# Layer 0 of a two-layer transformer kernel: a new order of its pieces on five engines, with two pieces moved between engines

## What is computed

```python
x = x + tanh(g_xattn[0]) * L0_xattn(layernorm(x), ctx, masks, Wq, bq, Wk, bk, Wv, bv, Wo, bo)
x = x + tanh(g_ffn[0])   * L0_ffn(layernorm(x), w_up, w_down)
x = x + tanh(g_xattn[1]) * L1_xattn(layernorm(x), ctx, ...)
x = x + tanh(g_ffn[1])   * L1_ffn(layernorm(x), Wr, Win, Wout)

def L0_ffn(h, w_up, w_down):
    h = square(relu(hbitlinear(h, w_up)))
    return hbitlinear(h, w_down)
def hbitlinear(x, w):                       # fwht: a Hadamard transform
    return act_quant(fwht(x)) @ weight_quant(w).T
def act_quant(x):                           # per token, to 8 bits: "the grid"
    scale = 127 / max(abs(x)); return clip(round(x * scale), -127, 127) / scale
```

## Time and profile before

| | us |
|---|---|
| median of 3 executions (1254.0 to 1259.59) | 1256.76 |
| the profiled execution | 1250.93 |
| its span, first to last instruction | 1249.2 |
| PE / DVE / ACT / POOL busy in it | 1119.2 / 1024.9 / 944.2 / 748.0 |
| layer 0: start of F2 of the first and of the last row | 72.99 and 313.27 |

### The profile page before, as it was taken

One profiled execution on the slowest core, in us unless ns is written; L12 is line 12 of the kernel. 1 busy time (PEld: TensorE's weight loads), 2 busy tenths in 40 slices (PEclk: granted clock), 3 DMA queues, 4 the chain that ended last, 5 costly groups with the idle time before them and its releaser, 6 DMA issues. The chain is left out here.

```text
span 1249.2 us, 30643 instructions
## 1 busy us (share of the span) xinstructions
PE 1119.2 (90%) x8831; PEld 906.0 (73%) x8831; DVE 1024.9 (82%) x2453; ACT 944.2 (76%) x3793; POOL 748.0 (60%) x1142
## 2 busy tenths in 40 slices
PE   3589899978899999999999999998999999669992
PEld 2356566545788888888888888887887888559981
DVE  6678888887898898898889899888789887766664
ACT  4777788869999989989998998997888778223330
POOL 5378888867665665666566566665546787323331
PEclk8699999999999999999999999999999999879996
DMA  6655555531220230220221121122311010623326
GB/s 132 131 90 92 90 88 86 83 53 53 89 73 2 90 90 0 89 89 16 72 89 33 56 89 51 38 89 70 92 51 48 31 36 31 276 80 94 88 69 206
DMA packets 134168, 97.57 MB, mean 78 GB/s; under 512 B 54845, under 2 KB 127679, under 8 KB 134080
## 3 DMA queue, kind: packets, MB, share of 16 engines
q1 hardware_dynamic: 124528, 84.70, 27.0%
q0 software_dynamic: 3408, 8.45, 1.9%
q10 hardware_dynamic: 6144, 3.35, 0.9%
HBM read 55.02 MB, written 42.09 MB: 78 GB/s over the span
## 5 line engine op out<-in xcount | busy, mean ns | idle before, releaser
L1557 POOL TENSOR_TENSOR head_rstd<-head_rstd,minus_half 128x4 f32<-128x4 f32 x192 | 225.7, 1175 | 15.0
L1545 ACT ACTIVATE squares<-ps 128x128 bf16<-128x128 f32 x768 | 202.5, 285 | 42.3 <-PE ps L1508 35.1
L1508 PE MATMUL ps<-w_proj_in,xq 128*128 128x512 f16 (+1 forms) x1024 | 209.6, 327 | 6.0 <-ACT headsT L1581 5.4
L1637 POOL TENSOR_TENSOR prob<-prob,rinv 128x512 f32<-128x512 f32 x128 | 140.5, 1098 | 107.6 <-DVE rinv L1632 107.4
L1581 ACT ACTIVATE headsT<-ps,l_hln 128x256 f32<-128x256 f32 (+1 forms) x256 | 168.2, 691 | 29.3 <-PE ps L1572 29.2
L1624 ACT ACTIVATE prob<-ps,nmax 128x128 f32<-128x128 f32 x512 | 182.7, 392 | 9.2 <-DVE nmax L1615 7.8
L1545 ACT ACTIVATION_READ_ACCUMULATOR squares<-ps 128x1 f32 x768 | 165.4, 216 | 0.0
L1565 DVE TENSOR_TENSOR heads_n<-ps,head_rstd 128x512 f32<-128x512 f32 x192 | 131.1, 683 | 25.0 <-POOL head_rstd L1557 24.8
L1508 PEld LDWEIGHTS ps<-w_proj_in,xq 128*128 (+1 forms) x1024 | 99.9, 98 | 53.1 <-issue 8.8
L1608 PE MATMUL ps<-headsT 128*128 128x128 f32 x1024 | 136.2, 276 | 1.0 <-DVE probT L1653 0.4
L1555 POOL TENSOR_TENSOR head_rstd<-head_squares,l_head_eps 128x4 f32<-128x4 f32 x192 | 45.8, 238 | 151.9 <-ACT squares L1545 151.2
(11 more groups left out here) (321 smaller groups left out, 2611.3 us busy)
## 6 DMA issues: line engine op xcount, KB each, us to landing
slots<-blank_slot SPq DMA_DIRECT2D x12, 1554.0 KB, 8.0
halves<-half_made SPq DMA_DIRECT2D x32, 256.0 KB, 2.6
w_proj_in<-halves SPq DMA_DIRECT2D x16, 512.0 KB, 9.3
w_out_raw<-in_wprojT SPq DMA_DIRECT2D x8, 512.0 KB, 4.0
half_raw<-in_winT SPq DMA_DIRECT2D x16, 256.0 KB, 3.0
half_raw<-in_woutT SPq DMA_DIRECT2D x16, 256.0 KB, 3.1
taken<-slots SPq DMA_DIRECT2D x15, 259.0 KB, 3.5
q_rows<-q_parts SPq DMA_DIRECT2D x48, 64.0 KB
```

Source lines behind the costliest of these rows:

```text
L1508: last = e.matmul(out, xq[:, k, which, slot_at], weights(k, hl, c0, n), start=(k == 0 and hl == 0), stop=(k == KD - 1 and hl == 1))
L1545: last = e.activation(squares[:, 4 * n + h, :], A[n][:, h * HD1:(h + 1) * HD1], ACT.Square, scale=HD1**-0.5, accum_out=hss[:, 4 * n + h:4 ...
L1557: e.tensor_tensor(hr[:, four], hr[:, four], t["half"][:, four], ALU.pow).then_inc(g_r[n].sem, 1)
L1637: e.tensor_tensor(prob[:, kind, :, :], prob[:, kind, :, :], spread(rinv[:, kind, :], P), ALU.mult).then_inc(g_p[kind].sem, 1)
```

## The change

All orders in `ORDER0` are new. XB moves to a later place on GpSimd, F4v to a place behind F1g. F5v, WL and WC, which were one piece each, become two pieces each, with the same instructions. F6q keeps the four steps of the scale on VectorE; the two roundings become a new piece F6r on ScalarE, two activations with a wait between them. WM moves from ScalarE, where it was twelve instructions, to VectorE, where it is one reduction; it no longer writes to `w_proj_in` and no longer waits for WL. F7s waits for the scale instead of the rounded values. `starting` names other pieces for some of the first work, and the strings in `MIXED` are new.

```diff
 ORDER0 = {
     "tensor": (
-        "PV:2- PV:3- NT ST:5- P2t++ F6--- ST:6- OB:0- F2t-- ST:7- P3++ S:0+ F3-- PV:4- PV:5- PV:6- PV:7- ST:0 "
-        "S:1+ ST:1 S:2+ F4-- ST:2 OB:1- F4u-- S:3+ ST:3 S:4+ OT- ST:4 S:5+ F7--- W- S:6+ S:7+ F7d--- PV:0 "
-        "PV:1"
+        "P2t++ PV:2- S:7 PV:3- ST:5- F6--- ST:6- NT OB:0- P3++ ST:7- F2t-- S:0+ S:1+ PV:4- F3-- PV:5- PV:6- PV:7- "
+        "ST:0 ST:1 S:2+ OB:1- F4-- S:3+ F4u-- ST:2 S:4+ OT- ST:3 S:5+ F7--- W- PV:0 S:6+ ST:4 PV:1 F7d---"
+    ),
+    "vector": (
+        "MX:5+ Wv- MX:6+ F1- F7v--- MX:7+ WM++ F2- F6q-- NTl+ P1++++ NO:0 MX:0++ MX:1++ F3q- P3v+++ MX:2++ NO:1 "
+        "MX:3++ MX:4++ P2++++"
     ),
     "scalar": (
-        "EX:5 P2a+++ F2a- EX:6 EX:7 WM:0++ P3h+++ WM:1++ OC:1 EX:0+ EX:1+ F4a- EX:2+ F4s- OTa WH++ F7a-- EX:3+ NTh++ EX:4+ "
+        "P2a+++ EX:5 NTh+ EX:6 F2a- F6r-- EX:7 P3h+++ OC:1 EX:0+ F4a- EX:1+ F4s- OTa EX:2+ F7a-- EX:3+ EX:4+ WH++ "
         "OC:0+"
     ),
-    "vector": (
-        "MX:5+ Wv- MX:6+ MX:7+ F1- F7v--- NTl+ F2- F6q-- NO:0 P1++++ MX:0++ F3q- P3v+++ MX:1++ MX:2++ "
-        "NO:1 MX:3++ MX:4++ P2++++"
-    ),
-    "gpsimd": "XB+ F5v-- F1g- WL+ F3b- VC++ PD+ P1g++++ WC++ F7s-- F4v-",
+    "gpsimd": "F5v:0-- F5v:1-- F1g- F4v-- WL:0+ WL:1+ F3b- XB+ VC++ WC:0++ P1g++++ WC:1++ PD++ F7s--",
     "sync": "INS- ROW-- INT- LW OUT CT++",
 }
...
     @s.piece("F3", "tensor")
     def _(e, i, p):
         e.wait_ge(g_sum.sem, g_sum.at(i))
-        e.wait_ge(v_q2.sem, v_q2.at(i - 1))
+        e.wait_ge(a_g2.sem, a_g2.at(i - 1))
...
+    @s.piece("F6r", "scalar")
+    def _(e, i, p):
+        e.wait_ge(c_f6.sem, c_f6.at(i))
+        e.activation(rnd2[:, :], F1[:, :], ACT.Copy, bias=MAGIC, scale=quant[:, p, 6:7]).then_inc(a_g2.sem, 1)
+        e.wait_ge(a_g2.sem, a_g2.at(i, 1))
         e.wait_ge(pe_q2.sem, pe_q2.at(i - 1))
-        quantise(e, c_f6, quant[:, p, :], F1[:, :], quant[:, p, 7:8], 4, rnd2[:, :], q2[:, :], v_q2)
-        c_f6.end()
+        e.activation(q2[:, :], rnd2[:, :], ACT.Copy, bias=-MAGIC).then_inc(a_g2.sem, 1)
...
-    @s.piece("WM", "scalar")
+    @s.piece("WM", "vector")
+    def _(e, i, p):
+        e.wait_ge(d_unit.sem, d_unit.at(i))
+        e.tensor_reduce(wsum[:, p, :], unit[:, p, 0:CENTRED * HD1].rearrange("p (h d) -> p h d", h=CENTRED),
+                        AX, ALU.add).then_inc(v_usum.sem, 1)
...
-            ("gpsimd", "P1g", 1, 1): ("blocks",), ("gpsimd", "VC", 0, 0): ("more", "masks"), ("gpsimd", "WC", 0, 0): ("ready",),
-            ("gpsimd", "XB", 0, 0): ("gated",),
+            ("gpsimd", "P1g", 1, 1): ("blocks",), ("gpsimd", "VC", 0, 0): ("more", "masks"), ("gpsimd", "WC", 0, 0, 0): ("ready",),
+            ("gpsimd", "PD", 0, 0): ("gated",),
...
-            ("vector", "P1", 1, 1): ("ready", "unit0", "more"), ("vector", "P2", 1, 1): ("unit1",), ("vector", "P1", 2, 0): ("masks",),
-            ("vector", "NTl", 1, 1): ("late",), ("vector", "NO", 0, 0, 0): ("late2",),
+            ("vector", "P1", 1, 1): ("ready", "unit0", "more"), ("vector", "P2", 1, 1): ("unit1",), ("vector", "WM", 0, 0): ("masks",),
+            ("vector", "MX", 1, 1, 5): ("late",), ("vector", "NO", 0, 0, 0): ("late2",),
```

More of the change, by code:

```diff
@@ L65, in link, with last, at @@
         self.engine.wait_ge(self.sem, self.i * self.per + self.n)
+    def last(self, instruction):
+        instruction.then_inc(self.sem, 1)
+        self.n += 1
+    def at(self, i):
+        return i * self.per + self.per
     def end(self):
@@ L1024, in quantise @@
         chain.link(e.reciprocal(quant[:, c + 1:c + 2], quant[:, c:c + 1]))
-        chain.link(e.tensor_scalar(quant[:, c + 2:c + 3], quant[:, c + 1:c + 2], norm, 127.0, ALU.mult, ALU.mult))
+        step = e.tensor_scalar(quant[:, c + 2:c + 3], quant[:, c + 1:c + 2], norm, 127.0, ALU.mult, ALU.mult)
+        if done is None:
+            chain.last(step)
+            return
+        chain.link(step)
         chain.link(e.tensor_scalar(rnd, src, quant[:, c + 2:c + 3], MAGIC, ALU.mult, ALU.add))
@@ L1081, in _ @@
     @s.piece("F5v", "gpsimd")
[L1082 to L1089, removed]
+    def _(e, i, p, n):
+        if n == 0:
+            e.wait_ge(a_hid.sem, a_hid.at(i))
+            e.tensor_tensor(fly[:, 0:4:2, :], hid[:, 0:4:2, :], hid[:, 1:4:2, :], ALU.add)
+            e.tensor_tensor(fly[:, 1:4:2, :], hid[:, 0:4:2, :], hid[:, 1:4:2, :], ALU.subtract).then_inc(g_fly.sem, 1)
+        else:
+            e.wait_ge(g_fly.sem, g_fly.at(i, 1))
+            e.wait_ge(pe_h2.sem, pe_h2.at(i - 1))
+            e.tensor_tensor(hidT[:, 0:2, :], fly[:, 0:2, :], fly[:, 2:4, :], ALU.add)
+            e.tensor_tensor(hidT[:, 2:4, :], fly[:, 0:2, :], fly[:, 2:4, :], ALU.subtract).then_inc(g_fly.sem, 1)
     @s.piece("F6", "tensor")
@@ L1152, in _ @@
             e.dma_start(unit[:, p, c0:c0 + w], a[name][p * P:(p + 1) * P, bass.ds(i * (w // 2) - p * (w // 2), w)]).then_inc(d_unit.sem, 16)
-    @s.piece("WM", "scalar")
+    @s.piece("WM", "vector")
[3 more added lines that the diff above has]
+                        AX, ALU.add).then_inc(v_usum.sem, 1)
+    @s.piece("WC", "gpsimd")
     def _(e, i, p, n):
         if n == 0:
[L1157 to L1174, removed]
+            e.wait_ge(v_usum.sem, v_usum.at(i))
+            e.tensor_tensor(wsum[:, p, :], wsum[:, p, :], share[:, :], ALU.mult).then_inc(g_unit.sem, 1)
+            e.wait_ge(g_unit.sem, g_unit.at(i, 1))
+            centred = unit[:, p, 0:CENTRED * HD1].rearrange("p (h d) -> p h d", h=CENTRED)
+            e.tensor_tensor(centred, centred, spread(wsum[:, p, :], HD1), ALU.subtract).then_inc(g_unit.sem, 1)
+        else:
+            e.wait_ge(g_unit.sem, g_unit.at(i, 2))
+            byhead = unit[:, p, :].rearrange("p (h d) -> p h d", d=HD1)
+            e.tensor_tensor(byhead, byhead, spread(wscale[:, p, :], HD1), ALU.mult).then_inc(g_unit.sem, 1)
     @s.piece("WH", "scalar")
@@ L1181, in _ @@
     @s.piece("WL", "gpsimd")
-    def _(e, i, p):
+    def _(e, i, p, n):
         e.wait_ge(a_uhigh.sem, a_uhigh.at(i))
         high, low = (t["wb"][:, hl, bass.ds(i, 1), :].rearrange("p u c -> p (u c)") for hl in (HI, LO))
-        for c0 in range(0, UNIT, UNIT // 4):
+        for c0 in range(n * UNIT // 2, (n + 1) * UNIT // 2, UNIT // 4):
             some = slice(c0, c0 + UNIT // 4)
@@ L2204 @@
     "tensor": (
-        "aaaaaaaaaaaaaaaaaaaaaaaaaaaaaaaabaaaaaaaaaabaaaaaaaaaaaaaaaaaaabaaaaaaaaaaabbaaaaabaaababaaabbababab"
-        "ababbbbabababbbbababbbbbbbbbbbbbbbbbbbbbbbbbbbbbbbbbbbb"
-    ),
[L2208 to L2211, removed]
+        "aaaaaaaaaaaaaaaaaaaaaaaaaaaaaaaaabaaaaaaaaaabaaaaaaaaaaaaaaaaaaabaaaaaaaaaaabbaaaaabaaababaaabbababa"
+        "bababbbbabababbbbababbbbbbbbbbbbbbbbbbbbbbbbbbbbbbbbbbbb"
+    ),
+    "vector": (
+        "aaaaaaaaaaaaaaaaaabbaaaaaaaaaaaaaabaaabaaaaaaaabaaaaabbbabbbaaaabaababbacbaaacaabbbabbbbbcbcbabbabbb"
+        "abbbbbbbbcbbbbbbbbcbbbbbbbbbbbbbbbbcbbbbbbbbbbbcbbbbbbb"
+    ),
+    "scalar": (
+        "aaaaaaaaaaaaaaaaaaaaaaaaaaaaaaaaaaaabbbaaaabaaaabaaabaabaabbaabcaaaabaaabababaababccbbbaacbbbbababaa"
+        "bbbccbbbabbbbbbbbbbcbbbbbbbbcbbbbbb"
+    ),
+    "gpsimd": (
+        "aaaaaaaaaaaaaabaaaaaaaaaaaaabaaaaaaaaabbaabaabababaaababaabbbaabbabbbbbbbbbbbbbbbbbbbbbbbb"
+    ),
+    "sync": (
+        "aaaaaaaaaaaaabaccccbccbcc"
+    ),
 }
```

20 lines of the change are left out of this document (11 added, 9 removed).

## The result

The changed kernel takes 1309.27 us (median of 4 runs, 1308.63 to 1309.98) against 1257.61 for the kernel before (the three executions above and one more): ratio 1.0414, 95% interval 1.0389 to 1.0440. The forecast was 1259.2 us with a range of 1250 to 1267. The profiled execution after took 1308.79 us, its span is 1307.0; before, 1250.93 and 1249.2, so these two differ by 57.8 us.

A forecast was written before the change was run, and what follows sets the result against it. The prediction took a loop of waits through GpSimd, TensorE and ScalarE to bound layer 0's rows (15.48 us). Eleven rows +1.2, ramp +1.2 and end 0 gave +2.4 on the 1256.76 median: 1259.2 us, range 1250 to 1267.

The forecast's parts named there:

- The matmuls are the same ones: TensorE's part in a row of layer 0: the change leaves its matmuls the same, only their order moves.
- one moves ahead of it (1.06 / 4 = 0.27 us): TensorE: one of four PV behind F3 moves ahead of it, so F3 to VC falls from 1.89 to 1.62 us.
- VC to F6 becomes 8.01: GpSimd: XB and F4v leave the stretch between VC and F5v, so VC to F6 falls from 9.10 to 8.01 us.
- The loop: Layer 0: waits through GpSimd, TensorE and ScalarE, once per row, set its length: 9.10 + 6.38 = 15.48 us.
- F6 to F2a 4.24, F3 at F6 + 5.96: TensorE and ScalarE: F2t behind P3 makes F6 to F2a 4.24 us (was 2.06); F3 comes 1.72 later (was F6 + 4.49).
- What GpSimd saves, the place of P3 takes back: Sum for a layer 0 row: 15.59 us against 15.48, in eleven rows +1.2 us, bounds -1.5 to +3.4.
- WM goes: 3.0 us a row: ScalarE: WM's twelve instructions, 3.0 us a row, leave and F6r adds 1.34; the 1.7 us become idle time.
- the ramp's +1.2: Before the first row's F2, VectorE has WM and P1 ahead of NO:0: +1.2 us, between 0 and 2.5.
- The end of layer 0: 0: Last rows, where pieces of both layers alternate: taken as 0 us, with bounds -3 and +4.
- ScalarE becomes the bound where the layers overlap: Slower rival, last four rows: F6r adds 4 x 1.34 = 5.4 us, in all +7.8, 1264.6 us; chance 0.17.
- ROW lands too late: Slower rival: SyncE's ROW transfers move later and TensorE waits before ST:0 in eleven rows, +7.9, 1264.7 us; chance 0.08.
- The faster rival: The engines' load, not the loop, sets the pace: a row of 15.0 us, in all -6.9, 1249.9 us; chance 0.14.

The follow-up runs named there:

- after_fours: The changed kernel with TensorE's PV:0 to PV:3 in one run and PV:4 to PV:7 in another, as before had them; 1278.24 us, ratio 1.0186 to before.
- before_split: The kernel before with TensorE's PV alone parted as in the changed kernel, six stretches a row instead of two; 1301.34 us, ratio 1.0372.
- before_xb: The kernel before with GpSimd's order alone changed: XB behind F3b, F4v behind F1g; 1250.98 us, ratio 0.9969.
- fours_f2t: fours_pool_act2 with F2t ahead of ST:7 and P3 again on TensorE, as in before; 1262.41 us, ratio 1.0057 to before.
- fours_pool: after_fours with layer 1's pieces ahead of both halves of F5v on GpSimd, where the layers alternate; 1266.57 us, ratio 1.0087 to before.
- fours_pool_act: fours_pool with the last F6r (row 15) two pieces later on ScalarE; 1267.93 us, ratio 1.0093 to before.
- fours_pool_act2: fours_pool with the last F6r (row 15) six pieces later on ScalarE; 1264.11 us, ratio 1.0066 to before.

## Why the prediction was wrong, step by step

- **"The matmuls are the same ones"** is the step that failed, and with it "one moves ahead of it (1.06 / 4 = 0.27 us)". The matmuls are the same, their cost isn't: it depends on their neighbours. The last line of the earlier trace rows had it, 8 matmuls of 128x512 in 1.06 us, and the view by line gives 604 ns for one of them: 8 x 0.604 = 4.8 us of records in 1.06. That alone isn't proof of work side by side (F6's eight records of 275 ns overlap too, 2.2 us in 1.06), but a PV alone can't take less than one record, 0.6 us. I divided a stretch by its members and took the quotient for the price of a member. It is the whole stretch: a PV alone 0.98 us, not 0.27. Four stretches more are 3.9 us; 3.0 of them arrived in the row. This is 31.0 of the 51.7 us taken out of after (after_fours), and 46.9 us put into before (before_split).
- The Trainium skill says it in words (TensorE: Matmul & The Clock Gate, section "Why this matters for your kernels"): small matmuls whose outputs lie in different groups of 32 partitions run concurrently, each in its own group of columns. The trace agrees (0.98 us for one, 0.99 for four). It would have been the rule to weigh here.
- **"VC to F6 becomes 8.01"**: VC to the end of F5v is 7.89 in after, 7.98 in before_xb. The size was right, but F6 doesn't follow F5v any more: TensorE's order holds it in after, VectorE's F7v in before_xb. The loop named only one of the two that F6 waits for; the other, F7v, ends 0.18 us before F6 starts in before. "F6 not waiting for F5v" was named as a sign against the forecast, and it came.
- **"F6 to F2a 4.24, F3 at F6 + 5.96"**: 4.08 and 5.85 (225.34 to 231.19) in after, 4.53 and 6.29 in after_fours. Right, and F6r, not F3b, is the last link, at 1.77 us behind F2a (forecast 1.72).
- **"What GpSimd saves, the place of P3 takes back"**, a row of 15.59: with PV in fours it is 16.14. F3 to F6 is 9.82 us there against the forecast's 9.63 (8.01 + 1.62), F6 to F3 6.29 against 5.96. Undoing P3's place brings F3 1.29 us forward, so the step's direction was right; only 0.18 a row is left of it, as F3q's last step then runs beside GpSimd's WC and takes 1 us longer (fours_f2t).
- **"WM goes: 3.0 us a row"** on ScalarE was mis-sized, by the same fault in the other direction: durations of records that overlap were added. Three pairs of WM take 0.90 us by their starts (before_xb, 217.11 to 218.01), six 1.8. ScalarE is busy 11.86 us in a row of after_fours, not 10.3. It cost the sum nothing, since ScalarE isn't the bound in a row.
- **VectorE**: WM takes 0.94 us (forecast 0.95). The first NO:0 is at 61.97 in after_fours (61.42 before), the first F6 0.7 us later; in the three other kernels with the same ramp (fours_pool and the two fours_pool_act) F6 is 0.3 to 1.8 us later, so the ramp's +1.2 was fair. In after it is at 63.71, and F6 5.6 us late; in before_split 63.23 and 7.1: PV again.
- **"The end of layer 0: 0"** failed. "Layer 1's pieces between the same neighbours, except that one falls between the halves of F5v" was read too lightly: it is not one but eight of them, in five rows, and a piece behind the half of F5v that waits also waits. 11.7 us. The last F6r does the same on ScalarE: put later it shortens the tail by 5.0 us (fours_pool_act2), of which 2.5, not clear of the noise, came back in the time.
- **The rivals.** "ScalarE becomes the bound where the layers overlap" had the place right, but not the mechanism, and that its 5.4 us are near the 5.0 of the tail is luck: ScalarE isn't full, it stands in front of F6r with layer 1's pieces behind it. "ROW lands too late" is out: the transfers start 2.8 us after F6 (209.33), and TensorE has no wait in front of ST:0 (213.98), nor in after_fours (225.66). The faster rival is out by a wide margin for the whole change; GpSimd's order alone is 0.3% faster (before_xb), but without the rival's row of 15.0.
- **What stays open**: fours_f2t still stands 0.6% above before. Its row is 0.18 us longer (1.8 us over ten), end and tail 6.5 us by the profiles, with the clock at 0.92 in the end (0.96 before); which pieces of the last rows these are, I did not separate.

## To carry to other kernels

Where an instruction's mean duration times its number is several times the busy time of its line, its price may lie in the group: look what keeps the group together before an order parts it, and until a lone member is measured, from its start to the next one's, price it at the whole stretch. The fault runs both ways: durations of overlapping records must not be added; take the distance from start to start. Where an order of pieces is changed, the pieces that wait are to be followed first: whatever stands behind them on their engine waits with them, and a piece cut in two so that others may pass must not have its waiting half in front. And where a step moves, see which instructions have changed their length beside their new neighbours before the order is blamed or cleared.
